# Picking 1024 columns by one-hot products: data as weights against table as weights (last layer of a two-layer Perceiver block on one core)

## The chip, the cores and the metric

The kernel runs on one core of a Trainium2 chip. The metric is the device time of one execution in microseconds (us). Its engines are TensorE (PE in the profile; its weight loads are shown apart as PEld), VectorE (DVE), ScalarE (ACT), GpSimd (POOL) and the DMA queues, which SyncE (SP) mostly issues.

## What is computed

The input `x` is 2 x 64 tokens of 1024 numbers, held as 128 rows. Five sublayers with a residual each go before the one that this document is about: a quantised product with the context, a state-space layer, a linear layer with low-rank experts, a cross attention and a self attention. The sixth and last is this, cut from the reference (`perm` is a random permutation of the 1024 columns, and the input is `_layernorm(x)`):

```python
def _L1_ffn_ref(x, up, down, perm):          # b*l = 128, h = 16 heads, d = 64, m = 256
    unperm = jnp.argsort(perm)
    t = x.reshape(b * l, Dm)
    t = t[:, perm]
    t = t.reshape(b * l, h, d)
    t = jnp.einsum('bhd,hdm->bhm', t, up)
    t = jax.nn.gelu(t, approximate=False)
    t = jnp.einsum('bhm,hmd->bhd', t, down)
    t = t.reshape(b * l, h * d)
    t = t[:, unperm]
    return t
x = x + _L1_ffn_ref(_layernorm(x, axis=-1), L1_ffn_up, L1_ffn_down, L1_ffn_perm)
```

## The kernel before

Each engine has its own program, written out by hand in one order, and the engines meet through semaphores (`wait_ge` waits, `then_inc` signals). TensorE computes `lhsT.T @ rhs`: the second argument of `pe.matmul` is loaded as weights, the third is the moving data, whose columns stream through. PSUM has 8 banks of 512 fp32 columns, written `psum[:, bank, :]`.

The last sublayer begins when `add_to_x` (L1491, DVE) has added the self attention's output to `x`, in two halves of 512 columns. Then, in the order of the work:

- `center` (L1496, DVE) subtracts the mean and writes `h`. PE turns `h` in 8 transposes of 128 x 128 (`transpose_h(5)`, a helper whose instructions carry L969) into banks 6 and 7, so that a bank holds column tiles of `h` on partitions and the 128 tokens along the columns.
- Since a product in fp32r keeps fewer bits than fp32, the turned data is kept as a sum of two fp32r parts, `split[:, 0]` (high, `left_high`, ACT L698) and `split[:, 1]` (low, `left_low`, DVE L1561), each 8 tiles of 128 columns by 128 tokens.
- Meanwhile `variance(5)` (DVE L1475, L1506, L1507) and `rstd_of(5)` (POOL L574) find `rstd`, one number per token. The normalisation is applied after the pick, since a scale per token and a choice of columns can change places.
- **The pick.** `onehot` is a table of 8 tiles, 128 rows (source columns) by 1024 (picked columns), made long before by DVE (L1859). PE forms `psum[token, picked] = sum over tiles of split.T @ onehot` (L1423): for each half `nh` of the picked columns 8 products with the high part and 8 with the low, 128 tokens as weights and 512 table columns moving, into banks 4 and 5. 32 products in all.
- The result stands with tokens on partitions, so it has to be turned again. ACT (L950, half 0) and DVE (L1964, half 1) copy it to `picked`, times `rstd` on the way, which is one number per partition here. PE transposes 4 tiles of each half (L969), and ACT (L952) and DVE (L1966) copy the turned halves to `gT`.
- `up`: 32 positions in `gT` and the weights, two halves of the array each, 64 products of 64 x 128 (L1439) into banks 0 to 7. The first 32 need `g_lo`, the others `g_hi`. Gelu on ACT (L958), then 64 `down` products (L1447) into banks 0 and 1, which are split again in two fp32r parts (ACT L961, DVE L1976, L1974).
- While that runs, DVE writes the second table over the first (L1969, 8 instructions; it must wait for the pick to be done), and 32 placing products (L1458), of the pick's shape, put the columns back. DVE adds them to `x` (L1985) and two DMAs write the output.

`idle_products` (L975) are products of the identity with itself whose results nobody reads. They stand where PE would otherwise wait.

Of the kernel before, what the change touches and what calls it, by code (L numbers as in the profile page):

```python
# [12 lines left out]
ALU = mybir.AluOpType  # L13
ACT = mybir.ActivationFunctionType
# [7 lines left out]
P = 128  # L22
B, L = 2, 64
D = 1024
KT = D // P
UK = 4
UN = 512
# [62 lines left out]
def perceiver(nc, dram, out):  # L90
# [7 lines left out]
    with ExitStack() as stack:  # L98
        def sb(name, shape, dtype=F32):
            return stack.enter_context(nc.sbuf_tensor(name, shape, dtype))  # L100

        def sem(name):
            return stack.enter_context(nc.semaphore(name))
# [5 lines left out]
        ident = sb("ident", [P, P])  # L109
# [4 lines left out]
        arena = sb("arena", [P, 24576])  # L114
# [4 lines left out]
        split = sb("split", [P, 2, KT, P], F32R)  # L119
        psum = stack.enter_context(nc.psum_tensor("psum", [P, 8, 512], F32))  # L120

        def carve(tile, start, *dims):
            size = 1
            for d in dims:
                size *= d
            ap = tile[:, start:start + size]
            if len(dims) == 2:
                ap = ap.rearrange("p (a b) -> p a b", a=dims[0])
            if len(dims) == 3:
                ap = ap.rearrange("p (a b c) -> p a b c", a=dims[0], b=dims[1])  # L130
            return ap
# [13 lines left out]
        rstd = carve(small, 89, 6)  # L145
# [109 lines left out]
        onehot = carve(arena_r, 15488, KT, D)  # L255
        gT = carve(arena, 0, KT, P)
        hidden = carve(arena, 1024, MH, 2, P)
        picked = carve(arena, 5120, D)
        y_out = carve(arena, 6144, D)


# [23 lines left out]
        rstd_ready = sem("rstd_ready")  # L285
# [119 lines left out]
        pick_ready = sem("pick_ready")  # L405
        place_ready = sem("place_ready")
        g_psum = sem("g_psum")
        picked_lo = sem("picked_lo")
        picked_hi = sem("picked_hi")
        gT_turned = sem("gT_turned")  # L410
        g_lo = sem("g_lo")
        g_hi = sem("g_hi")
        up_psum = sem("up_psum")
# [59 lines left out]
        def place(n):  # L473
            if slot_of[n] > SLOTS:
                return ring_spare[:, slot_of[n] - SLOTS - 1, :]
            return ring_more if slot_of[n] == SLOTS else ring[:, slot_of[n], :]
# [40 lines left out]
        def wide(ap, count):  # L517

            n = ap.shape[1]
            return ap.rearrange("p (u n) -> p u n", u=1).to_broadcast([P, count, n])  # L520
# [143 lines left out]
        def _(act):  # L664
# [16 lines left out]
            for n in range(8):  # L681
# [7 lines left out]
                for cols in code_parts(n):  # L689
                    act.activation(ctx_code[:, n % 2, cols], ring[:, slot_of[n], cols], ACT.Identity, bias=quant[:, 3:4],  # L690
                                   scale=qrec[:, 1:2]).then_inc(ctx_scaled, 1)
# [225 lines left out]
            for r in range(GQ):  # L917
                last = act.activation(krep[:, :, r, :], krot.rearrange("p (g d) -> p g d", g=HKV), ACT.Copy, scale=rstd[:, 4:5])
# [26 lines left out]

            left_high(hT_psum, 10)
            act.preload_act_table_set("gelu_and_others")
            act.wait_ge(g_psum, 1)
            act.wait_ge(rstd_ready, 6)
            act.activation(picked[:, 0:UN], psum[:, 4, :], ACT.Copy, scale=rstd[:, 5:6]).then_inc(picked_lo, 1)  # L950
            act.wait_ge(gT_turned, 1)
            act.activation(gT[:, 0:4, :], psum[:, 6, :], ACT.Copy).then_inc(g_lo, 1)  # L952
            for q in range(4):
                for r in range(2):

# [8 lines left out]
        def _(pe):  # L964
            def transpose4(bank, tile, first_col, signal):

                for k in range(4):
                    c = first_col + P * k
                    last = pe.transpose(psum[:, bank, P * k:P * k + P], tile[:, c:c + P], ident[:, :])  # L969
                last.then_inc(signal, 1)  # L970
# [11 lines left out]
            for nh in range(2):  # L982
                for kh in range(2):
                    for b in range(B):
# [3 lines left out]
                        for k in range(UK):  # L988
# [7 lines left out]
                            last = pe.matmul(psum[rows, 2 + nh, :], ones64, right, **at)  # L996
                last.then_inc(q_done, 1)
            for k in range(UK // 2, UK):
                last = pe.matmul(psum[L:P, 1, :], q1T[:, UK + k, L:P], q2[:, 7, UN * k:UN * k + UN], start=False,
                                 stop=(k == UK - 1))  # L1000
# [256 lines left out]
            for k in range(KT):  # L1257
                last = pe.matmul(psum[:, 4, 0:NE * RANK + NE], hT[:, k, :], w_ar[:, k, :], start=(k == 0), stop=(k == KT - 1))
# [156 lines left out]
            idle_products(0, 4)  # L1415
            transpose_h(5)
            pe.wait_ge(pick_ready, KT)
            for nh in range(2):
                for part, signal in enumerate((hs_high, hs_low)):
                    for k in range(KT):  # L1420
                        if nh == 0 and k % 4 == 0:
                            pe.wait_ge(signal, 9 + k // 4)
                        last = pe.matmul(psum[:, 4 + nh, :], split[:, part, k, :], onehot[:, k, UN * nh:UN * nh + UN],  # L1423
                                         start=(part == 0 and k == 0), stop=(part == 1 and k == KT - 1))
                last.then_inc(g_psum, 1)
            for half in range(2):
                pe.wait_ge(picked_hi if half else picked_lo, 1)
                transpose4(6 + half, picked, UN * half, gT_turned)
            up = place(first["mlp_up"]).rearrange("p (a m) -> p a m", a=MH // 2)
            down = place(first["mlp_down"]).rearrange("p (m h d) -> p m h d", m=2, h=MH)  # L1430
            arrived(pe, first["mlp_up"])
# [1 line left out]
            for a in range(MH // 2):  # L1433
                pe.wait_ge(g_hi if a >= 4 else g_lo, 1)
                for m in range(2):
                    for r in range(2):
                        rows = slice(MD * r, MD * r + MD)
                        at = 256 * (a % 2) + P * m
                        last = pe.matmul(psum[:, 4 * r + a // 2, at:at + P], up[rows, a, P * m:P * m + P], gT[rows, a, :],  # L1439
                                         start=True, stop=True)  # L1440
                if a % 2:
                    last.then_inc(up_psum, 1)
            for a in range(MH // 2):
                pe.wait_ge(hidden_ready, 2 * (a // 2 + 1))
                for m in range(2):
                    for r in range(2):
                        last = pe.matmul(psum[MD * r:MD * r + MD, a // 4, P * (a % 4):P * (a % 4) + P], down[:, m, 2 * a + r, :],  # L1447
                                         hidden[:, 2 * a + r, m, :], start=(m == 0), stop=(m == 1))
                if a % 4 == 3:
                    last.then_inc(down_psum, 1)  # L1450
            for nh in range(2):
                for part, signal in enumerate((o_high, o_low)):
                    for k in range(KT):
                        if nh == 0 and k % 4 == 0:
                            pe.wait_ge(signal, k // 4 + 1)
                        if nh == 0 and part == 0:
                            pe.wait_ge(place_ready, k + 1)
                        last = pe.matmul(psum[:, 2 + nh, :], split[:, part, k, :], onehot[:, k, UN * nh:UN * nh + UN],  # L1458
                                         start=(part == 0 and k == 0), stop=(part == 1 and k == KT - 1))
# [3 lines left out]
        def _(dve):  # L1463
# [7 lines left out]
            def halves(nh):  # L1471
                return slice(UN * nh, UN * nh + UN)
# [16 lines left out]
            def add_to_x(nh, bank, factor=1.0):  # L1489

                dve.scalar_tensor_tensor(out=x[:, halves(nh)], in0=psum[:, bank, :], scalar=factor, in1=x[:, halves(nh)],  # L1491
                                         op0=ALU.mult, op1=ALU.add, accum_out=x_sum[:, nh:nh + 1]).then_inc(x_ready, 1)
                updates[0] += 1
                dve.wait_ge(x_ready, updates[0])
# [6 lines left out]
            def variance(n):  # L1501

                statistics(0)
                statistics(1)
                dve.wait_ge(stats_ready, 2 * n + 2)
                step(dve.bn_aggr(mv, stats.rearrange("p a b -> p (a b)")))  # L1506
                dve.tensor_scalar(var_eps, mv[:, 1:2], LN_EPS, None, ALU.add).then_inc(var_ready, 1)  # L1507
# [135 lines left out]
            for i, (a, c) in enumerate(parts):  # L1643
                last = dve.tensor_scalar(rms_var[:, i:i + 1], rms_sum[:, i:i + 1], 1.0 / (c - a), RMS_EPS, ALU.mult, ALU.add)
# [308 lines left out]
            low(25)  # L1953
            for nh in range(2):
                dve.wait_ge(ao_psum, nh + 1)
                add_to_x(nh, 4 + nh)


            center()
            left_low(10)  # L1960
            variance(5)
            dve.wait_ge(g_psum, 2)
            dve.wait_ge(rstd_ready, 6)
            dve.tensor_scalar(picked[:, halves(1)], psum[:, 5, :], rstd[:, 5:6], None, ALU.mult).then_inc(picked_hi, 1)  # L1964
            dve.wait_ge(gT_turned, 2)
            dve.tensor_copy(gT[:, 4:8, :], psum[:, 7, :]).then_inc(g_hi, 1)  # L1966

            for k in range(KT):
                dve.tensor_scalar(onehot[:, k, :], iota, perm_col[:, k:k + 1], None, ALU.is_equal).then_inc(place_ready, 1)  # L1969
# [93 lines left out]
```

## Time and profile before

| | us |
|---|---|
| median of 3 runs (359.96 to 360.26) | 360.2 |
| the profiled execution, its own time | 359.97 |
| its span, first to last instruction | 358.1 |
| PE busy in it | 323.7 (90%) |
| DVE busy | 268.1 (75%) |
| ACT busy | 205.4 (57%) |

The profile describes one execution. Its span is 1.9 us shorter than the time of the same execution, which holds what lies around the instructions. A busy time of an engine adds the stretches in which it worked on something; a matmul's recorded length contains the trip of the data through the array, so a row of matmuls overlaps itself and its pace has to be read from start to start. "idle before" is how long an engine sat before the instruction, and "<-" names what ended that.

### The profile page before, as it was taken

The numbers are of one execution on the slowest core, as the hardware profiler recorded it, in microseconds if no ns is written. First come the engines' busy times: TensorE is split into PE (matmuls) and PEld (weight loads), VectorE is DVE, ScalarE is ACT, GpSimd is POOL, SyncE is SP. The second block draws the span as 40 slices with busy tenths as digits, with TensorE's granted clock in tenths as the row PEclk, the third lists the DMA queues.
The fourth block names the chain that finished last, engine by engine and source line by source line (L and its number), as shares of the span: only waits on it lengthen the run. The fifth ranks groups of instructions, "written<-read, shape, count | busy, mean of one in ns | idle before, by whom it ended". The sixth has DMA issues, their size and how long they took to land.

```text
span 358.1 us, 5132 instructions
## 1 busy us (share of the span) xinstructions
PE 323.7 (90%) x1944; PEld 214.5 (60%) x1944; DVE 268.1 (75%) x369; ACT 205.4 (57%) x402; POOL 108.7 (30%) x75
## 2 busy tenths in 40 slices
PE   0697999999789999999899898999999999898996
PEld 0344564654456566667548776785343777777794
DVE  1877787768788999999594998995423898875381
ACT  1984644168999999997425735651024566451250
POOL 2510100042987999999200020202000110400000
PEclk9999999999999999999999999999999999999999
DMA  6999999945003021363579696789999993000001
GB/s 238 424 423 417 422 319 420 385 158 195 12 0 118 2 71 49 118 240 117 165 285 372 254 422 263 282 348 373 417 425 357 428 419 137 4 2 0 0 2 59
DMA packets 12966, 81.85 MB, mean 229 GB/s; under 512 B 2109, under 2 KB 2365, under 8 KB 3661
## 3 DMA queue, kind: packets, MB, share of 16 engines
q1 hardware_dynamic: 11614, 78.23, 55.9%
q10 hardware_dynamic: 1296, 3.22, 2.6%
q8 instruction: 15, 0.25, 0.3%
q14 instruction: 9, 0.07, 0.1%
q0 software_dynamic: 32, 0.07, 0.1%
HBM read 80.86 MB, written 0.52 MB: 227 GB/s over the span
## 4 chain that ended last, share of the span: by engine, by line
PE 44%; DVE 16%; ACT 2%; issue 2%; POOL 1%; DVEq 0%
PE psum L1012 8%; PE psum L1304 8%; PE psum L1019 4%; PE psum L1189 4%; PE psum L1149 4%; DVE rounded L1752 4%; PE psum L1224 3%; PE psum L1073 3%; PE psum L969 2%; PE psum L1423 2%; PE psum L1458 2%; DVE arena L1690 1%; DVE arena_halves L1760 1%; PE psum L1439 1%; PE psum L1447 1%
## 5 line engine op out<-in xcount | busy, mean ns | idle before, releaser
L800 ACT ACTIVATE arena<-arena 128x126 f32<-128x126 f32 x256 | 75.9, 392 | 0.3 <-DVE plain L1690 0.3
L635 POOL TENSOR_TENSOR arena<-arena 128x1024 f32<-128x1024 f32 x21 | 49.7, 2377 | 11.8 <-DVE arena L1690 10.7
L1690 DVE TENSOR_TENSOR_SCAN arena<-arena,psum 128x1024 f32<-128x1024 f32 x22 | 49.7, 2275 | 1.7 <-PE psum L1149 1.3
L1073 PE MATMUL psum<-ring,hT 128*128 128x512 f32 x104 | 50.2, 605 | 0.8 <-ACT hT L701 0.8
L574 POOL TENSOR_TENSOR small<-small 128x1 f32<-128x1 f32 x6 | 9.6, 1607 | 135.0 <-DVE small L1507 129.4
L1752 DVE TENSOR_TENSOR rounded<-ring,rounded 128x2048 fp32r<-128x2048 f32 x16 | 36.5, 2286 | 15.0 <-ACT rounded L827 15.0
L827 ACT ACTIVATE rounded<-ring 128x2048 fp32r<-128x2048 f32 x16 | 30.6, 1913 | 17.5 <-PE psum L1019 9.5
L1189 PEld LDWEIGHTS psum<-ident,arena 128*128 128x128 f32 x256 | 28.9, 141 | 12.5 <-issue 12.1
L1189 PE MATMUL psum<-ident,arena 128*128 128x128 f32 x256 | 33.6, 275 | 0.0
L1149 PE MATMUL psum<-rounded 64*128 64x512 f32 x192 | 30.9, 426 | 1.7 <-DVE arena L1690 1.0
L1073 PEld LDWEIGHTS psum<-ring,hT 128*128 128x128 f32 x104 | 17.8, 190 | 17.6 <-issue 16.4
L1012 PE MATMUL psum<-rounded,split 128*128 128x512 f32 x96 | 24.6, 399 | 2.4 <-DVE rounded L1752 1.8
L1304 PE MATMUL psum<-ring,arena 128*64 128x512 f32 x96 | 24.4, 593 | 0.0
L635 POOL TENSOR_TENSOR arena<-plain,arena 128x1024 f32<-128x1024 f32 x10 | 23.7, 2374 | 0.9 <-DVE plain L1690 0.7
L1690 DVE TENSOR_TENSOR_SCAN plain<-arena,psum 128x1024 f32<-128x1024 f32 x10 | 22.8, 2276 | 0.4 <-ACT arena L800 0.3
L969 PE MATMUL psum<-ident,arena 128*128 128x128 f32 x120 | 18.7, 280 | 4.0 <-DVE arena L1662 1.7
L1149 PEld LDWEIGHTS psum<-rounded 64*128 64x128 f32 x192 | 15.6, 185 | 10.7 <-issue 5.2
L1012 PEld LDWEIGHTS psum<-rounded,split 128*128 128x128 f32 x96 | 17.5, 188 | 7.5 <-DVE rounded L1752 2.9
L690 ACT ACTIVATE arena<-ring,small 128x2048 uint8<-128x2048 f32 (+1 forms) x9 | 16.9, 1900 | 7.9 <-DMA ring<-in_ctx 7.9
L969 PE MATMUL psum<-ident,h 128*128 128x128 f32 x48 | 7.4, 304 | 15.1 <-DVE h L1518 11.7
L969 PEld LDWEIGHTS psum<-ident,arena 128*128 128x128 f32 x120 | 13.4, 140 | 11.7 <-issue 6.0
L827 ACT ACTIVATE arena_halves<-ring 128x2048 fp32r<-128x2048 f32 x8 | 15.3, 1917 | 6.1 <-PE psum L1019 5.6
(238 smaller groups left out, 574.9 us busy)
## 6 DMA issues: line engine op xcount, KB each, us to landing
ring<-in_w_in SPq DMA_DIRECT2D x16, 1024.0 KB, 15.2
ring<-in_ctx SPq DMA_DIRECT2D x13, 1024.0 KB, 10.2
ring<-in_w_out SPq DMA_DIRECT2D x8, 1024.0 KB, 5.1
ring<-in_ctx_t SPq DMA_DIRECT2D x7, 1024.0 KB, 5.6
ring<-in_w_base SPq DMA_DIRECT2D x4, 1024.0 KB, 4.9
ring<-in_x_wk SPq DMA_DIRECT2D x4, 1024.0 KB, 10.2
ring<-in_a_wo SPq DMA_DIRECT2D x4, 1024.0 KB, 11.8
ring<-in_x_wq SPq DMA_DIRECT2D x3, 1024.0 KB, 9.0
```

The lines of the kernel that those rows point to most:

```text
L635: pool.tensor_tensor(product[s % STATES].rearrange("p (n b t) -> p b n t", n=HN, b=B), state[s % STATES].rearrange("p (b n t) -> p b n t", ...
L690: act.activation(ctx_code[:, n % 2, cols], ring[:, slot_of[n], cols], ACT.Identity, bias=quant[:, 3:4], scale=qrec[:, 1:2]).then_inc(ctx_s ...
L800: last = act.activation(to, of, ACT.Exp, scale=a_par[:, k, state_no:state_no + 1])
L827: act.activation(unit_halves[m % 3][:, 0, :, :], slot(split_units[m]), ACT.Copy).then_inc(unit_high, 1)
L969: last = pe.transpose(psum[:, bank, P * k:P * k + P], tile[:, c:c + P], ident[:, :])
L1012: pe.matmul(psum[:, bank, :], left(0, k0 + k), unit[:, w, k, :], start=(start and k == 0 and w == 0), stop=False)
L1073: last = pe.matmul(psum[:, proj_bank(j), :], hT[:, k, :], slot(w_in + u)[:, k % UK, :], **at)
L1149: last = pe.matmul(psum[:, input_bank(s, b), :], du[k // GD][rows_of(b), a, left], bdiag[rows_of(b), w, right, :], start=(n == 0), stop=(n ...
L1189: last = pe.matmul(psum[:, y_bank(q), to:to + P], product[s % STATES][:, P * n:P * n + P], ident[:, :], start=(s % 2 == 0 and n == 0), sto ...
L1304: last = pe.matmul(psum[L * b:L * b + L, bank, :], left[:, UK * kh + k, L * b:L * b + L], slot(u0 + b)[:, k, :], start=(kh == 0 and k == 0 ...
L1690: dve.tensor_tensor_scan(state[s % STATES], dA[:, s % 3, :], psum[:, p:p + 2, :].rearrange("p a b -> p (a b)"), 0.0, ALU.mult, ALU.add).th ...
L1752: dve.tensor_tensor(unit[:, 1, :, :], slot(split_units[m]), unit[:, 0, :, :].bitcast(F32), ALU.subtract).then_inc(unit_low, 1)
```

## The change

The operands of the pick change places. A table tile of 128 x 128 is now the weights, and the turned data (one tile of 128 tokens) moves through it. What comes out stands already turned, with picked columns on partitions and tokens along the columns. So `picked`, its two scaled copies and the 8 transposes go, and for each half, part and tile there are now 4 products of 128 columns in place of 1 of 512: 128 in all, into banks 2 and 3.

The scale `rstd` now belongs to a column, not to a partition. DVE writes a diagonal of it (`rstd_diag`, from the identity), PE multiplies a 128 x 128 matrix of ones with it (one product into bank 7, between the halves of the pick), ACT copies the result to `rstd_wide`, and DVE multiplies each half of the pick by it on the way to `gT`. The ones are written by a memset on DVE before the first `add_to_x`.

```diff
-            for nh in range(2):
+            for half in range(2):
                 for part, signal in enumerate((hs_high, hs_low)):
                     for k in range(KT):
-                        if nh == 0 and k % 4 == 0:
+                        if half == 0 and k % 4 == 0:
                             pe.wait_ge(signal, 9 + k // 4)
-                        last = pe.matmul(psum[:, 4 + nh, :], split[:, part, k, :], onehot[:, k, UN * nh:UN * nh + UN],
-                                         start=(part == 0 and k == 0), stop=(part == 1 and k == KT - 1))
+                        for m in range(4):
+                            of = UN * half + P * m
+                            last = pe.matmul(psum[:, 2 + half, P * m:P * m + P], onehot[:, k, of:of + P], split[:, part, k, :],
+                                             start=(part == 0 and k == 0 and m == 0), stop=(part == 1 and k == KT - 1),
+                                             skip_group_check=True)
                 last.then_inc(g_psum, 1)
-            for half in range(2):
-                pe.wait_ge(picked_hi if half else picked_lo, 1)
-                transpose4(6 + half, picked, UN * half, gT_turned)
+                if half == 0:
+                    pe.wait_ge(diag_ready, 2)
+                    pe.matmul(psum[:, 7, 0:P], all_ones, rstd_diag, start=True, stop=True).then_inc(g_psum, 1)
...
             left_high(hT_psum, 10)
             act.preload_act_table_set("gelu_and_others")
-            act.wait_ge(g_psum, 1)
-            act.wait_ge(rstd_ready, 6)
-            act.activation(picked[:, 0:UN], psum[:, 4, :], ACT.Copy, scale=rstd[:, 5:6]).then_inc(picked_lo, 1)
-            act.wait_ge(gT_turned, 1)
-            act.activation(gT[:, 0:4, :], psum[:, 6, :], ACT.Copy).then_inc(g_lo, 1)
+            act.wait_ge(g_psum, 2)
+            act.activation(rstd_wide, psum[:, 7, 0:P], ACT.Copy).then_inc(wide_ready, 1)
...
                 dve.wait_ge(ao_psum, nh + 1)
+                if nh == 0:
+                    dve.memset(all_ones, 1.0).then_inc(diag_ready, 1)
                 add_to_x(nh, 4 + nh)
...
             variance(5)
-            dve.wait_ge(g_psum, 2)
             dve.wait_ge(rstd_ready, 6)
-            dve.tensor_scalar(picked[:, halves(1)], psum[:, 5, :], rstd[:, 5:6], None, ALU.mult).then_inc(picked_hi, 1)
-            dve.wait_ge(gT_turned, 2)
-            dve.tensor_copy(gT[:, 4:8, :], psum[:, 7, :]).then_inc(g_hi, 1)
+            dve.tensor_scalar(rstd_diag, ident[:, :], rstd[:, 5:6], None, ALU.mult).then_inc(diag_ready, 1)
+            for half in range(2):
+                if half == 0:
+                    dve.wait_ge(wide_ready, 1)
+                else:
+                    dve.wait_ge(g_psum, 3)
+                dve.tensor_tensor(gT[:, 4 * half:4 * half + 4, :], psum[:, 2 + half, :].rearrange("p (m t) -> p m t", m=4),
+                                  wide(rstd_wide, 4), ALU.mult).then_inc(g_hi if half else g_lo, 1)
```

PE's rows before, from the last products of the self attention to the placing products:

```order
L975 MATMUL psum<-ident 128x128 x4
L969 MATMUL psum<-ident,h 128x128 x8
L1423 MATMUL psum<-arena_halves,split 128x512 x32
L969 MATMUL psum<-ident,arena 128x128 x8
L1439 MATMUL psum<-arena,ring 128x128 x32
```

The same place with the change (lines of PE's program stand 2 lower up to the pick, 1 higher behind it):

```order
L973 MATMUL psum<-ident 128x128 x4
L967 MATMUL psum<-ident,h 128x128 x8
L1423 MATMUL psum<-split,arena_halves 128x128 x64
L1429 MATMUL psum<-arena 128x128
L1423 MATMUL psum<-split,arena_halves 128x128 x64
L1440 MATMUL psum<-arena,ring 128x128 x32
```

Forty instructions (32 products, 8 transposes) became 129, all of 128 moving columns, and each has a weight load of 128 columns.

DVE before, from `variance(5)` to the second table, with the semaphores that it waits on:

```order
L1507 TENSOR_SCALAR small<-small 128x1 [waits dve_step]
L1964 TENSOR_SCALAR arena<-psum,small 128x512 [waits rstd_ready,g_psum]
L1966 COPY arena<-psum 128x512 [waits gT_turned]
L1969 TENSOR_SCALAR arena_halves<-arena,small 128x1024 x8
L1976 TENSOR_TENSOR split<-psum,split 128x512 [waits o_high]
```

And with the change:

```order
L1508 TENSOR_SCALAR small<-small 128x1 [waits dve_step]
L1966 TENSOR_SCALAR arena<-ident,small 128x128 [waits rstd_ready]
L1972 TENSOR_TENSOR arena<-psum,arena 128x512 [waits wide_ready]
L1972 TENSOR_TENSOR arena<-psum,arena 128x512 [waits g_psum]
L1976 TENSOR_SCALAR arena_halves<-arena,small 128x1024 x8
L1983 TENSOR_TENSOR split<-psum,split 128x512 [waits o_high]
```

DVE now writes both halves of `gT`, and the second table comes behind one instruction that follows the pick where two did.

## Rows read from the trace of the kernel before

**Rows 1.** The page: busy times, granted clock, chain that ended last

```profile
PE 323.7 (90%) x1944; PEld 214.5 (60%) x1944; DVE 268.1 (75%) x369; ACT 205.4 (57%) x402; POOL 108.7 (30%) x75
...
PEclk9999999999999999999999999999999999999999
```

**Rows 2.** Chain of waits, end of the kernel: start us, us, what

```profile
328.00 0.71 DVE x L1491 x2
...
329.53 0.67 PE psum L969 x4
...
330.22 0.61 ACT split L698
...
330.96 7.55 PE psum L1423 x32
...
338.54 0.76 DVE arena L1964
...
339.35 0.66 PE psum L969 x4
340.00 3.77 PE psum L1439 x64
...
347.42 7.50 PE psum L1458 x32
```

**Rows 3.** Timeline, 318 to 359 us: start us, us, instruction [idle before]

```profile
325.20 0.69 DVE L1491 SCALAR_TENSOR_TENSOR x<-psum,x 128x512 f32<-128x512 f32 x1 [1.15 <-PE psum L1019]
...
328.00 0.69 DVE L1491 SCALAR_TENSOR_TENSOR x<-psum,x 128x512 f32<-128x512 f32 x1 [2.10 <-PE psum L1019]
...
330.96 7.54 PE L1423 MATMUL psum<-arena_halves,split 128*128 128x512 f32 x32 [0.34 <-ACT split L698]
...
333.84 0.55 POOL L574 TENSOR_TENSOR small<-small 128x1 f32<-128x1 f32 x1 [21.66 <-DVE small L1507]
...
339.93 3.84 PE L1439 MATMUL psum<-arena,ring 64*128 64x128 f32 x64
340.04 0.69 DVE L1966 COPY arena<-psum 128x512 f32<-128x512 f32 x1 [0.75 <-PE psum L969]
340.65 5.39 DVE L1969 TENSOR_SCALAR arena_halves<-arena,small 128x1024 fp32r<-128x1024 f32 x8
...
346.42 0.69 DVE L1976 TENSOR_TENSOR split<-psum,split 128x512 fp32r<-128x512 f32 x1 [0.38 <-ACT split L961]
```

**Rows 4.** Timeline of PE, 66 to 72 and 200 to 318 us

```profile
67.21 2.81 PE L1089 MATMUL psum<-arena 128*128 128x96 f32 x24
...
207.42 2.02 PE L1258 MATMUL psum<-arena,hT 128*128 128x136 f32 x16
217.90 1.05 PE L975 MATMUL psum<-ident 128*128 128x128 f32 x8
...
306.04 2.05 PE L975 MATMUL psum<-ident 128*128 128x128 f32 x16
```

**Rows 5.** Groups by line and shape, PEld: busy us, mean ns | idle before

```profile
L1012 PEld LDWEIGHTS psum<-rounded,split 128*128 128x128 f32 x96 | 17.5, 188 | 7.5 <-DVE rounded L1752 2.9 <-ACT split L698 1.2
...
L969 PEld LDWEIGHTS psum<-ident,arena 128*128 128x128 f32 x120 | 13.4, 140 | 11.7 <-issue 6.0 <-ACT arena L937 1.3 <-ACT arena L902 1.0
...
L1089 PEld LDWEIGHTS psum<-arena 128*128 128x128 f32 x32 | 3.9, 192 | 1.0 <-issue 0.6 <-DVE arena L1618 0.3
```

**Rows 6.** One line each: durations ns min/median/max, first and last start us

```profile
L878 ACT ACTIVATE arena<-psum x1: 277/277/277, 214.8 to 214.8; 128x128 f32<-128x128 f32 x1
...
L1713 DVE SCALAR_TENSOR_TENSOR arena<-arena,small,psum x16: 322/340/346, 115.0 to 182.3; 128x128 f32<-128x128 f32 x16
...
L995 PEld LDWEIGHTS psum<-arena x30: 106/110/178, 14.5 to 28.8; 128*64 128x64 bf16 x30
```

**Rows 7.** Stretches: us, busy (x) of PE, PEld, DVE, ACT, POOL, PEclk, DMA, GB/s

```profile
300.00:307.00 7.00, 6.72 (x153) 5.78 (x152) 6.70 (x10) 1.44 (x2) 0.00 (x0) 1.00 0.02 5
...
331.00:338.50 7.50, 7.50 (x34) 6.16 (x35) 2.69 (x6) 2.28 (x3) 0.55 (x1) 1.00 0.00 0
```

More of the change, by code:

```diff
@@ L257, in perceiver @@
         hidden = carve(arena, 1024, MH, 2, P)
-        picked = carve(arena, 5120, D)
+        all_ones = carve(arena, 5120, P)
+        rstd_diag = carve(arena, 5248, P)
+        rstd_wide = carve(arena, 5376, P)
         y_out = carve(arena, 6144, D)
@@ L407, in perceiver @@
         g_psum = sem("g_psum")
-        picked_lo = sem("picked_lo")
-        picked_hi = sem("picked_hi")
-        gT_turned = sem("gT_turned")
+        diag_ready = sem("diag_ready")
+        wide_ready = sem("wide_ready")
         g_lo = sem("g_lo")
```

## The prediction

> **What bounds the kernel now.** I read the page first. PE is busy for 90% of the span and the granted clock is at its full level in every slice, which is the 2.4 GHz one of TensorE's two levels [rows 1]. A busy share does not say which engine ends a stage, so the next view is the chain of waits over the last sublayer [rows 2]. The reader is to see that it is one string without gaps: DVE adds and centres, PE turns `h` (0.67 us), ACT makes the high part (0.61), PE picks (7.55 from 330.96), DVE scales the second half (0.76), PE turns it (0.66), then the `up` products start (340.00) and, behind the `down` products, the placing products (7.50 from 347.42). The timeline has the first `up` product at 339.93 [rows 3]; I count from this time. From the first picking product to the first `up` product it is **339.93 - 330.96 = 8.97 us**, and this is the piece that the change rewrites. No transfer ends a wait in this piece, and nothing before it or behind it in PE's order is edited.
>
> **What the change takes away.** The second scaled copy, the second four transposes and the steps between go from the chain. The pick's last product ends at 338.52 (330.96 + 7.55, rounded), so this is 339.93 - 338.52 = 1.4 us. The first half's copy and transposes were hidden behind PE and DVE already and are worth nothing by themselves. If 128 products took as long as 32 did, the change would win these 1.4 us.
>
> **What a product costs now.** The question is the pace of a 128-column load followed by a product of 128 moving columns in fp32r. No row of before has that pair, so I bound it.
>
> - The old products run at (7.54 - 0.39)/31 = 0.23 us from start to start (0.39 is the recorded length of one) [rows 3]. That is 512 columns of data, and the load was hidden behind them. A quarter of it, 0.057 us, is what 128 columns would take if only the moving data counted: the **lower end**.
> - Products in fp32 with 128-column loads show what the load does. 24 products with 96 moving columns take 2.81 us: (2.81 - 0.275)/23 = 0.110 each. 8 with 128 columns: (1.05 - 0.275)/7 = 0.111. 16 with 136 columns: (2.02 - 0.279)/15 = 0.116 [rows 4]. From 128 to 136 the pace grows with the data. From 96 to 128 it does not: fewer columns bought nothing. Something that does not depend on the moving data takes 0.110 us, and what these three have in common is the load of 128 fp32 columns.
> - Is a load of fp32r as dear as one of fp32? Their records are as long: 188 ns on average for fp32r tables and data, 192 for fp32 [rows 5]. The record follows the work: a bf16 load of 64 columns has a median of 110 ns [rows 6] and the load of a transpose 140 ns [rows 5]. So a shorter load would be seen, and fp32r does not show one. I take **0.110 us** for a pair: the moving part (0.057) hides behind the load, where before the load hid behind the moving part.
> - The upper end. If load and moving part could not overlap, a pair would take 0.110 + 0.057 = 0.167 us. If a short product cost as much as a long one whatever its columns, it would be 0.23.
>
> Nearest among these is the row of 96 columns, a full-width load with less moving work than load work, which is the new pair's situation. A stretch of 16 idle products runs at (2.05 - 0.275)/15 = 0.118 [rows 4], so the pace of long runs is not always the best one; I allow 0.105 to 0.122.
>
> **The sum.** 128 picking products and the product of ones are 129 pairs: 129 x 0.110 = 14.2 us, in place of 8.97. The first `up` product then starts at 345.15 instead of 339.93: **+5.2 us**. Everything else I cost at nothing on this path, for these reasons.
>
> - The memset of `all_ones` is one small DVE instruction ahead of the first addition. The second addition starts at 328.00 after 2.10 us of idle time [rows 3], so DVE has the room. Without that room it would delay `center` by its own length, and with it the pick.
> - The diagonal: POOL's `rstd` is ready at 333.84 + 0.55 = 334.39 [rows 3]. DVE's scaling of the identity has the size of the 128 x 128 operation at 0.34 us [rows 6], so it is ready at about 334.8. PE asks for it after 64 products, at 330.96 + 7.04 = 338.0. There is no wait. At a pace under 0.06 there would be one of some 0.2 us.
> - ACT's copy to `rstd_wide` is like the 128 x 128 copy at 0.28 us [rows 6], and DVE's multiplication of the first half takes about 0.75 us, as its other PSUM operations of this size with an operand do [rows 2]. Both lie under the second half of the pick. The first half of `gT` is ready at about 339.4, well before 345.15.
> - The second half of `gT` is late by design: DVE starts it when the last picking product ends, about 0.16 us after the first `up` product starts, and is done 0.95 us after that start. Only the 33rd `up` product needs it, which comes after half of 3.84 us, 1.9 us. It is hidden.
> - The second table: DVE wrote it from 0.72 us to 6.11 us after the first `up` product [rows 3]. Now it goes from 0.95 to about 6.35. The next DVE step, the subtraction for the low part, came at 346.42, 6.49 us after the first `up` product, because it waited for ACT. The margin is 0.14 us; a worse DVE delay would be paid once, at its own size.
> - ACT's and DVE's other savings (L952, L966's place, L950) free engines that are not what PE waits for.
>
> A rule of the Trainium skill speaks for the change. "TensorE: Matmul & The Clock Gate", section "Weight-path perf modes — Fast Weight Load (FWL) and DoubleRow", says that loads of 128 weights in a type other than fp32 take a fast path, about twice as quick. By it a pair would take about 0.057 us and the sum would be a gain of 1.4 us. The equal records of fp32r and fp32 above are why the forecast does not go by it.
>
> **The numbers.** The sum is made on the profiled execution: 358.1 + 5.2 = 363.3 us of span, 359.97 + 5.2 = 365.2 us of time. That execution is 0.2 us under the median of the runs shown, so the median should come out at 360.2 + 5.2 = **365.4 us**. The allowance of 0.105 to 0.122 gives 13.5 to 15.7 us, or +4.6 to +6.8: 364.8 to 367.0. Differences under 0.2%, 0.7 us, can't be told from no change.
>
> **The rivals.**
>
> - *The load hides too (faster).* The mechanism is a quick load of fp32r tables in front of 128-column products. The `up` products show such a pace, (3.84 - 0.27)/63 = 0.057 us a product with 128-column loads [rows 3], but there two halves of the array take turns, and here each product needs the whole array. The first half would end at 334.6, the product of ones would wait for the diagonal until 334.8, and the second half would end at 334.8 + 65 x 0.057 = 338.5: 1.4 us earlier, **358.8 us**. It decides from a pace of 8.97/129 = 0.070 us downward. For it speaks that 512-column products say nothing on a load's true price, only that it is under 0.23. Against it stand the records of 188 ns. Chance 12%.
> - *Half-way.* The load is partly quicker, with a pace in the middle between 0.057 and 0.110, 0.084 us: 129 x 0.084 = 10.8 us, +1.9, **362.1 us**. Chance 6%. The same page of the Trainium skill, section "Back-to-back issue gap", gives about 81 ns for a load and a product of 128 columns, which would make it 361.7 us.
> - *No overlap.* Every table tile has to be in the whole array before its data moves, and the next load waits until the data is through: 129 x 0.167 = 21.5 us, +12.6, **372.8 us**. Against it: fp32 products of 128 columns have at least as much moving work and run at 0.111, which leaves no room for a sum. Chance 6%. The same page of the Trainium skill, section "The mechanism", says that a load overlaps running products only when its row group differs, which would give this case; the rows just named speak against it.
> - *A short fp32r product is as dear as a long one.* 129 x 0.23 = 29.7 us, +20.7, **380.9 us**. No fp32r product with under 512 moving columns is in the trace, so nothing excludes it, but fp32 ones got cheaper with their columns. Chance 5%.
> - *The clock falls.* PE moves fewer columns per us in the new stretch. In 300 to 307 us, 153 products, most of 64 columns, ran with the full clock granted [rows 7], as the old pick did. At the lower level the tail behind the pick would take up to twice as long. Chance 1%.
>
> **How the numbers follow.** The forecast, a pace set by the load, has 70%. The range reaches from the half-way case with its rounding, 361.3, to the case without overlap, 373.0. It leaves out the faster case (12%) and the two dearest (6%). Faster by over 0.2% is the first rival and a little of the half-way one, 13%; within 0.2% is a pace of 0.064 to 0.075, 2%; slower is the rest, 85%.
>
> **What would show it.** In the profile after: 128 products at the pick's line over about 14.1 us, load records still near 188 ns and nearly back to back, the first `up` product near 345.1, clock 1.00 throughout. The product of ones should show no wait for DVE, ACT's copy of it should lie under the pick, and from the first `up` product to the end everything should look as before, with the same 18.1 us. If the pick's products come at 0.06 us, the step from the load records to the load's price was wrong; if they come well above 0.12, either the overlap or the price of short fp32r products was. If the pace is right and the time is not, the tail behind the first `up` product has grown, and the second table or the second half of `gT` is where to look.

## The result, and the profile after

The median of 4 runs with the change is 366.2 us (366.03 to 366.22), against 360.23 us (359.96 to 360.28) for 4 runs of the kernel before. The ratio is 1.0167, with a 95% interval from 1.0155 to 1.0178: **1.7% slower, 6.0 us**. The prediction said 365.4 us, in a range of 361.3 to 373.0.

The profiled execution of the changed kernel took 366.03 us, with a span of 364.0. Its page, the counterpart of [rows 1]:

```profile
span 364.0 us, 5311 instructions
...
PE 330.9 (91%) x2034; PEld 223.2 (61%) x2034; DVE 268.4 (74%) x371; ACT 204.4 (56%) x401; POOL 108.7 (30%) x75
...
PEclk9999999999989999999999999999999999999999
```

Read alone, these lines hide the change: PE's busy share went from 90% to 91%. The chain of waits from 329 us on (start us, us, what) shows where the time is; it answers [rows 2]:

```profile
329.76 0.67 PE psum L967 x4
...
330.45 0.60 ACT split L699
...
331.20 7.33 PE psum L1423 x64
338.53 0.27 PE psum L1429 x2
338.80 7.10 PE psum L1423 x64
345.90 3.77 PE psum L1440 x64
349.67 3.64 PE psum L1448 x64
353.32 7.48 PE psum L1459 x32
```

Before, the pick was one row of 7.55 us, followed by 0.76 on DVE and 0.66 of transposes. Now the last picking product is followed at once by the `up` products, as the change intends, but the two rows of the pick hold 14.4 us. The timeline of the changed kernel, 323 to 365 us, has the rest (it answers [rows 3]):

```profile
325.50 0.17 DVE L1958 MEMSET arena<- 128x128 f32 x1 [1.22 <-PE psum L1017]
...
328.24 0.69 DVE L1492 SCALAR_TENSOR_TENSOR x<-psum,x 128x512 f32<-128x512 f32 x1 [2.02 <-PE psum L1017]
...
331.17 7.22 PEld L1423 LDWEIGHTS psum<-split,arena_halves 128*128 128x128 f32 x64 [0.55 <-issue]
331.20 7.33 PE L1423 MATMUL psum<-split,arena_halves 128*128 128x128 f32 x64 [0.34 <-ACT split L699]
...
334.66 0.29 DVE L1966 TENSOR_SCALAR arena<-ident,small 128x128 f32<-128x128 f32 x1 [0.66 <-POOL small L575]
338.31 0.30 PEld L1429 LDWEIGHTS psum<-arena 128*128 128x128 f32 x2
338.37 0.44 PE L1429 MATMUL psum<-arena 128*128 128x128 f32 x2
...
338.84 0.28 ACT L950 ACTIVATE arena<-psum 128x128 f32<-128x128 f32 x1 [6.00 <-PE psum L1429]
339.15 0.69 DVE L1972 TENSOR_TENSOR arena<-psum,arena 128x512 f32<-128x512 f32 x1 [4.20 <-ACT arena L950]
345.83 3.65 PEld L1440 LDWEIGHTS psum<-arena,ring 64*128 64x128 f32 x64
345.83 3.84 PE L1440 MATMUL psum<-arena,ring 64*128 64x128 f32 x64
345.94 0.69 DVE L1972 TENSOR_TENSOR arena<-psum,arena 128x512 f32<-128x512 f32 x1 [6.10 <-PE psum L1423]
346.55 5.38 DVE L1976 TENSOR_SCALAR arena_halves<-arena,small 128x1024 fp32r<-128x1024 f32 x8
```

Three readings. The loads (PEld) stand as long as the products, 7.22 beside 7.33 us: the load engine's record has no gap left. The pace is (7.33 - 0.28)/63 = 0.112 us. And from the first picking product to the first `up` product it is 345.83 - 331.20 = **14.63 us, against 8.97 before: 5.66 us** of the 5.9 by which the span grew. Behind that point nothing moved: 364.0 - 345.83 = 18.2 us, as before.

The other 0.24 us lie ahead of the pick. They came up between 102 and 199 us: a row of products of an earlier sublayer starts at 101.86 us here and at 101.89 before, an addition of DVE at 199.17 here and at 198.96 before. The change edits nothing there. The slice with an 8 in the clock's line is a short fall of the granted clock, which one row of the stretches places (us, busy of PE, PEld, DVE, ACT, POOL, PEclk, DMA, GB/s):

```profile
103.00:106.00 3.00, 3.00 (x13) 2.06 (x13) 1.42 (x2) 2.94 (x8) 1.09 (x2) 0.60 0.00 0
```

In this profile the clock was at the lower level for part of that stretch. The profile of before had 1.00 there, although PE had been busy for as long in 100 to 103 us (1.21 us before, 1.20 here). Of 11 runs of the kernel before, made beside a later experiment, 9 had a mean clock of 0.994 to 0.998 where its profile has 1.000, one had 1.000, and one had 0.947 and took 364.31 us. So the kernel before meets this fall too, and once a much longer one (an estimate from the mean: (1 - 0.947)/0.5 x 362.4 = 38 us at the lower level). The fall need not be all of the 0.24 us: a later version that kept a clock of 1.000 began its pick at 331.13 us, and another, which is the kernel before up to the pick, at 331.39.

### The profile page after: what moved, and what is told of

Its sections match the earlier page's. It is cut to its first block, busy times and chain, and to the rows that moved or that the text cites. A ratio compares the mean times of both kernels' runs of the same rounds, so it can differ in the third digit from the quotient of the medians.

```text
span 364.0 us, 5311 instructions
## 1 busy us (share of the span) xinstructions
PE 330.9 (91%) x2034; PEld 223.2 (61%) x2034; DVE 268.4 (74%) x371; ACT 204.4 (56%) x401; POOL 108.7 (30%) x75
## 4 chain that ended last, share of the span: by engine, by line
PE 59%; DVE 17%; issue 8%; ACT 7%; DMA 6%; POOL 2%; SPq 0%; DVEq 0%; ACTq 0%; POOLq 0%
PE psum L1010 8%; PE psum L1302 8%; PE psum L1071 7%; PE psum L1187 6%; DMA ring<-in_ctx 6%; PE psum L1147 6%; PE psum L1017 4%; PE psum L1423 4%; DVE rounded L1753 3%; PE psum L967 3%; PE psum L1222 3%; ACT arena L801 2%; PE psum L1459 2%; DVE arena L1691 2%; DVE arena_halves L1761 1%
```

## A correction to the counting ahead

The text ahead speaks of 64 `up` products and 64 `down` products. The loops make 32 of each, and the trace shows 64 records of each: a product of plain fp32 leaves two matmul records with two loads here. A product of fp32r leaves one record, and so does a transpose (8 for 8). `idle_products(0, 4)` is 8 records in the same way. The paces of [rows 4] are paces of records, each with its load, so the price of a load stands. The product of ones is fp32, though, and it is the row "L1429 ... x2" above. The prediction counted it once.

## The experiments

All seven leave the work ahead of the last sublayer as it is. The question is what the 0.112 us are the price of: the load, the moving columns, or a product as such. The first four were executed once each, beside one execution of the kernel before that took 360.5 us; they are read by their paces, and only roughly by their times.

**Half of the moving columns.**

```diff
-last = pe.matmul(psum[:, 2 + half, P * m:P * m + P], onehot[:, k, of:of + P], split[:, part, k, :],
+last = pe.matmul(psum[:, 2 + half, P * m:P * m + L], onehot[:, k, of:of + P], split[:, part, k, 0:L],
```

> The changed kernel, but each of the 128 picking products moves 64 tokens instead of 128; the weight load keeps its 128 columns. It leaves out the pick for the second batch. Theory (the load of 128 fp32r columns sets the pace): 0.112 us from start to start as in the changed kernel, time 366.2 us. Rival A (short fp32r products pay double per moving column, 128 of them 0.107 us, and the load hides behind): 0.055 us, 128 x 0.055 less, about 359 us. Rival B (a fixed price for every product, whatever its operands): 0.112 us and 366.2 us, as the theory.

Measured: 379.28 us, 13 us more than any theory gave. The stretches of this run (columns as above):

```profile
331.50:333.50 2.00, 2.00 (x19) 2.00 (x19) 2.00 (x4) 1.61 (x2) 0.00 (x0) 1.00 0.00 0
...
333.50:335.00 1.50, 1.50 (x14) 1.50 (x14) 0.77 (x4) 0.00 (x0) 0.55 (x1) 0.86 0.00 0
335.00:338.00 3.00, 3.00 (x16) 3.00 (x16) 0.24 (x1) 0.00 (x0) 0.00 (x0) 0.50 0.00 0
...
347.00:351.00 4.00, 4.00 (x20) 4.00 (x21) 0.00 (x0) 0.00 (x0) 0.00 (x0) 0.50 0.00 0
```

While the clock was at 2.4 GHz there were 19 products in 2.0 us, 0.105 us each (0.10 to 0.11, since whole products are counted): halving the moving columns bought next to nothing, so the moving part does not set the pace (rival A falls). Then, between 333.5 and 335 us, the granted clock went to 0.50, the 1.2 GHz level, and the pace to 4.0/20 = 0.20 us. The total time of this run is that of a lower clock and says nothing on the question; only the first 2 us do.

**Half of the loaded columns.**

```diff
-last = pe.matmul(psum[:, 2 + half, P * m:P * m + P], onehot[:, k, of:of + P], split[:, part, k, :],
+last = pe.matmul(psum[0:L, 2 + half, P * m:P * m + P], onehot[:, k, of:of + L], split[:, part, k, :],
```

> The changed kernel, but each picking product loads 64 table columns instead of 128 and moves 128 tokens. It leaves out half of the picked columns. Theory (the load sets the pace): the load halves, 0.055 to 0.06 us a product, 128 x 0.055 = 7 us less, about 359 us. Rival A (the moving part, double per column): 0.107 to 0.112 us, 366.2 us. Rival B (a fixed price): 0.112 us, 366.2 us.

Measured: 359.69 us, beside 360.5 us for the kernel before on the same chip. The chain of waits and the line's own view (ns min/median/max):

```profile
331.39 4.02 PE psum L1423 x64
335.41 0.28 PE psum L1429 x2
335.69 3.84 PE psum L1423 x64
```

```profile
L1423 PEld LDWEIGHTS psum<-split,arena_halves x128: 133/136/138, 331.4 to 339.2; 128*64 128x64 f32 x128
L1423 PE MATMUL psum<-split,arena_halves x128: 220/223/302, 331.4 to 339.3; 128*64 128x128 f32 x128
```

With the same 128 moving columns and the same number of products, 3.84/64 = 0.060 us each. Half the load, half the price, and nearly as low as the moving columns allow (the 0.057 us of the prediction's lower end). Rival A and rival B, the fixed price, both fall here.

**The same bytes as bf16.**

```diff
-last = pe.matmul(psum[:, 2 + half, P * m:P * m + P], onehot[:, k, of:of + P], split[:, part, k, :],
+last = pe.matmul(psum[:, 2 + half, P * m:P * m + P], onehot[:, k, of:of + L].bitcast(BF16),
+                 split[:, part, k, 0:L].bitcast(BF16),
```

> The changed kernel, but the same bytes are read as bf16: each product loads 128 bf16 columns and moves 128 bf16 columns, half of the bytes. The numbers picked are not the reference's. If the price of the load hangs on the type (a bf16 load of 64 columns was 110 ns long in the trace before where an fp32 one was 137): 0.055 to 0.06 us a product, about 359 us. If any load of 128 columns costs the same: 0.112 us, 366.2 us.

Measured: 359.36 us.

```profile
L1423 PEld LDWEIGHTS psum<-split,arena_halves x128: 95/98/100, 331.3 to 339.0; 128*128 128x128 bf16 x128
```

```profile
335.66 3.57 PE psum L1423 x64
```

128 columns loaded, 128 moved, and 3.57/64 = 0.056 us. So it is not the number of columns alone: the type, or the bytes behind it, halves the pace. Both operands changed here, but the moving one did not set the pace before. And 0.056 us is about the 0.057 that the prediction worked out for 128 moving columns by themselves, so it is the most that the bf16 load can cost; its own price may be lower. The load's record is 98 ns long, where the changed kernel has this:

```profile
L1423 PEld LDWEIGHTS psum<-split,arena_halves x128: 186/192/192, 331.2 to 345.6; 128*128 128x128 f32 x128
```

This is the pace that the prediction's first rival needed. It exists, for bf16. The fast path of the Trainium skill ("TensorE: Matmul & The Clock Gate", section "Weight-path perf modes — Fast Weight Load (FWL) and DoubleRow") is given there to loads of 128 weights in a type other than fp32. These two rows fit it if fp32r is counted as fp32; whether the bf16 loads took that path no row tells.

**The old roles, cut to 128 columns.**

```diff
-                        last = pe.matmul(psum[:, 4 + nh, :], split[:, part, k, :], onehot[:, k, UN * nh:UN * nh + UN],
-                                         start=(part == 0 and k == 0), stop=(part == 1 and k == KT - 1))
+                        for m in range(4):
+                            of = UN * nh + P * m
+                            last = pe.matmul(psum[:, 4 + nh, P * m:P * m + P], split[:, part, k, :], onehot[:, k, of:of + P],
+                                             start=(part == 0 and k == 0 and m == 0), stop=(part == 1 and k == KT - 1),
+                                             skip_group_check=True)
```

> The kernel before with its old roles (turned data as weights, table moving) and its transposes, but the 32 products of 512 table columns are cut into 128 products of 128, each with its own load. Theory (the load sets the pace, whichever operand is loaded): 0.112 us a product, 128 x 0.112 + 0.16 = 14.5 us in place of 7.55, 6.95 us slower than before: 367.2 us. Rival C (the load of the table is what is slow, since its rows are far apart, and a load of the data is quick): 0.057 us a product and 360.2 us.

Measured: 367.37 us, 6.9 us over the 360.5 us of the kernel before beside it, forecast 6.95. In its chain:

```profile
331.39 14.49 PE psum L1425 x128
...
345.91 0.76 DVE arena L1967
...
346.71 0.66 PE psum L969 x4
347.37 3.77 PE psum L1442 x64
```

The timeline shows a load for every product:

```profile
331.36 14.37 PEld L1425 LDWEIGHTS psum<-arena_halves,split 128*128 128x128 f32 x128 [0.55 <-issue]
```

The pace, (14.48 - 0.28)/127 = 0.112 us, is that of the changed kernel although the weights are the data, not the table, and although four products in a row load the same tile. What is loaded does not matter; that a load comes with every 128 moving columns does. This run also splits the change in its two effects: the cut from 32 to 128 products costs 6.9 us, and the new roles give 1.3 of them back (from the pick's start to the `up` products the chain has 15.98 us here and 14.70 in the changed kernel).

**Without the product of ones.** PE's product goes and ACT copies the diagonal itself.

```diff
-                if half == 0:
-                    pe.wait_ge(diag_ready, 2)
-                    pe.matmul(psum[:, 7, 0:P], all_ones, rstd_diag, start=True, stop=True).then_inc(g_psum, 1)
...
-            act.wait_ge(g_psum, 2)
-            act.activation(rstd_wide, psum[:, 7, 0:P], ACT.Copy).then_inc(wide_ready, 1)
+            act.wait_ge(g_psum, 1)
+            act.wait_ge(diag_ready, 2)
+            act.activation(rstd_wide, rstd_diag, ACT.Copy).then_inc(wide_ready, 1)
...
-                    dve.wait_ge(g_psum, 3)
+                    dve.wait_ge(g_psum, 2)
```

> The changed kernel without the product of ones: ACT copies the diagonal itself, so the scale is spread wrongly and the product's place in PE's order is empty. The product shows as two records and 0.27 us in the chain of waits, where the prediction had 0.11. Theory: 0.22 to 0.27 us faster than the changed kernel, 365.9 to 366.0 us. Rival (only one more pair at the load's pace): 0.11 us, 366.1 us.

Measured: 365.88 us (365.78 to 366.09, 6 runs), ratio to the kernel before 1.0147 (1.011 to 1.0183). In its chain the pick is one piece:

```profile
331.13 14.48 PE psum L1424 x128
345.61 3.77 PE psum L1438 x64
```

From the pick's start to the `up` products the chain has 14.48 us, against 345.90 - 331.20 = 14.70 with the product: 0.22 us, twice the prediction's 0.11. Between the medians it is 0.3 us, but the two were not taken beside each other.

**Both parts through one load.** If the load is the price, it should be used for more columns. Here each table tile is loaded once, and high and low part move through it side by side; DVE multiplies and adds the two. (A first version, in which one instruction of DVE was to read both parts from PSUM and add them, gave no time; here each part is multiplied by itself.)

```diff
+            def pick(m, k):
+                bank, at = PICK_AT[m]
+                return pe.matmul(psum[:, bank, at:at + 2 * P], onehot[:, k, P * m:P * m + P], split[:, :, k, :],
+                                 start=(at == 0 and k == 0), stop=(k == KT - 1), skip_group_check=True)
...
```

> The pick keeps the new roles, but each table tile is loaded once and both parts of the data move through it, high and low side by side, 256 columns: 64 products. They go to six banks; for each tile DVE multiplies both parts by the spread deviation and adds them. The second half is picked tile by tile, so that DVE follows. The pick can start only when the first low part is there, 0.7 us later. Theory (the pace is the dearer of a load of 128 fp32r columns, 0.112 us, and the moving part, 256 x 0.226/512 = 0.113 us): 64 x 0.113 = 7.2 us in place of 14.3, less the 0.7: about 6.4 us faster than the changed kernel, 359.8 us, 0.4 us under the kernel before, with 0.3 us of doubt for DVE's longer work at the end. Rival A (short fp32r products pay double per column): 64 x 0.213 = 13.6 us, about 366 us.

Measured: 360.39 us (359.89 to 361.62, 11 runs), ratio to the kernel before 1.0009 (1.0 to 1.0018): level with it, and 5.8 us under the changed kernel.

```profile
331.44 0.70 DVE split L1567
...
332.27 4.07 PE psum L1419 x32
336.35 0.22 PE psum L1430 x2
336.57 3.83 PE psum L1419 x32
340.40 3.87 PE psum L1445 x64
```

The later start is there (DVE's low part is now a step of the chain). The pace came out at 3.83/32 = 0.120 us, not 0.113: with 256 moving columns it is above the price of the load (0.112) and above that of the data (0.113). Why, no run shows. 64 x 0.007 = 0.4 us is the gain that was expected and did not come. Rival A's 366 us is far off.

**Each half in the roles that suit it.** The experiments point to a mixture. Half 0 keeps long products and hides its transposes; half 1, whose transposes nothing hides, takes the new roles with both parts through one load.

```diff
+                    last = pe.matmul(psum[:, 4, :], split[:, part, k, :], onehot[:, k, 0:UN],
+                                     start=(part == 0 and k == 0), stop=(part == 1 and k == KT - 1))
...
+            def pick(m):
+                for k in range(KT):
+                    last = pe.matmul(psum[:, PICK_BANK[m - 4], 0:2 * P], onehot[:, k, P * m:P * m + P], split[:, :, k, :],
+                                     start=(k == 0), stop=(k == KT - 1))
+                last.then_inc(g_psum, 1)
+
+            pick(4)
+            pe.wait_ge(diag_ready, 2)
+            pe.matmul(psum[:, 1, 0:P], all_ones, rstd_diag, start=True, stop=True).then_inc(g_psum, 1)
+            pick(5)
+            pe.wait_ge(picked_lo, 1)
+            transpose4(5, picked, 0, g_psum)
+            pick(6)
+            pick(7)
```

> Each half of the pick in the roles that suit it. Half 0 as in the kernel before (data as weights, 16 products of 512 table columns), so that its copy and its four transposes hide under the rest of the pick. Half 1 in the changed roles, tile by tile, with both parts of the data moving through one load (32 products of 256 columns), so that nothing has to be turned after the last product. The product of ones stands after tile 4, the transposes after tile 5. Theory, from measured paces: 16 x 0.226 + 32 x 0.121 + 0.25 for the product of ones + 4 x 0.11 for the transposes = 8.2 us from the first picking product to the first up product, where the kernel before has 8.97 and the changed kernel 14.63: 0.8 us faster than before, 359.4 us. Rival: the semaphore waits between the pieces, or DVE's three operations per tile and the later second table, eat it up: 360.2 us or more.

Measured: 359.52 us (359.29 to 360.27, 11 runs) against 360.36 us (15 runs) of the kernel before, ratio 0.9981 (0.9972 to 0.9990): 0.8 us faster, as forecast, and of the versions that do the whole work the only one that beats the kernel before. The gain is 0.2%, the size below which the prediction would call nothing a change, but these runs are many, taken beside each other, and the interval leaves out 1.

```profile
331.26 3.89 PE psum L1429 x16
335.15 0.95 PE psum L1435 x8
336.11 0.22 PE psum L1441 x2
336.33 0.95 PE psum L1435 x8
337.29 0.44 PE psum L976 x4
337.72 1.91 PE psum L1435 x16
339.64 3.77 PE psum L1457 x64
```

All of it is PE's own work, one piece behind the other, 8.38 us in this view where [rows 2] has 9.04; no wait for ACT or DVE came in between. So the pick itself gives 0.66 of the 0.84 us between the medians, a little less than the 0.8 forecast; the rest isn't traced.

## Why the prediction was right

- **What a product costs now.** The step that carried the forecast was that the load sets the pace at 0.110 us. It was 0.112, and the four tests of it agree: 0.105 with half of the moving columns, 0.060 with half of the loaded ones, 0.056 in bf16, and 0.112 with the operands in either role.
- **The equal records.** That fp32r loads cost what fp32 loads cost was argued from the length of their records, 188 and 192 ns. The conclusion held, and the two cheap loads have shorter records, 136 and 98 ns. But the length of a record does not give the pace by itself, and the trace of the kernel before could have shown it (the first line's numbers are ns min/median/max):

```profile
L1439 PEld LDWEIGHTS psum<-arena,ring x64: 183/188/189, 339.9 to 343.4; 64*128 64x128 f32 x64
...
338.34 0.60 PE L969 MATMUL psum<-ident,arena 128*128 128x128 f32 x4
```

The `up` loads, in turns into two halves of the array, have records of 188 ns at a pace of 0.057 us; the transposes, whose loads have 140 ns [rows 5], run at (0.60 - 0.273)/3 = 0.109 us, no quicker than products with loads of 192. Taken from the records alone the step would have been luck; the row of 96 moving columns and the experiments are what carry it.

- **The sum.** Forecast +5.2 us, measured 5.66 in the profile's piece. The terms that were mis-sized are two: the pace (128 x 0.002 = 0.26 us) and the product of ones, one pair at 0.110 in the sum and 0.22 to 0.27 in the traces, since it is fp32 and leaves two records. Together they make 0.4 of the missing 0.46 us.
- **The covers.** All held. The second addition still waited 2.02 us behind the memset (0.17 us), PE showed no wait for the diagonal (ready at 334.95, asked for at 338.3), both of DVE's multiplications were hidden, and the tail behind the first `up` product is 18.2 us as it was.
- **The median.** 366.2 against 365.4 us. 0.46 us of the gap are the terms above. The other 0.3 us lie outside the piece and stay open. They are of the size of the clock's fall near 105 us: of 15 later runs of the kernel before, 7 with a clock of 0.999 or 1.000 took 359.96 to 360.14 us and 8 with about 0.994 took 360.26 to 360.49. But the clocks of the four runs behind the 360.23 us are not known, and three of these four, at 360.20 to 360.28, look rather as if they had the fall as well.
- **The rivals.** The quick load did not come for fp32r and did for bf16, and there, as that rival had it, the product of ones had to wait for the diagonal (0.25 us). The half-way case and the 81 ns of the Trainium skill ("TensorE: Matmul & The Clock Gate", section "Back-to-back issue gap") fit neither type here: 112 ns in fp32r, 56 in bf16. No overlap (0.167) and the price of a long product (0.23) are excluded by 0.112. The clock did not fall in the changed kernel's pick. It did in the one run with 64 moving columns; the section on the hardware says how little one run shows of the cause.

## What to carry to other kernels

Count loads as well as products: in fp32r, a product with its own 128-column load took 0.112 us with 128 moving columns, 0.120 with 256 and 0.23 with 512, so the columns beyond the first 128 cost little up to 256. To swap the operands for a result that comes out turned pays only while each load still has enough columns behind it; where it has not, move more data through one load, or swap only the part whose transposes nothing hides. A busy share (90% to 91% here) does not see such a change; the distance between two named instructions does.

## What the runs showed of the hardware that I had not expected

- The granted clock fell while PE's records left no gap. With 128-column loads and 64 moving columns, PE and PEld were busy for all of 331.5 to 335 us, and between 333.5 and 335 the clock went to 0.50. It stayed there through the rest of the pick, which took 25 us in place of 14.6, and through the `up` products (6.32 us in the chain in place of 3.77). The same loads with 128 moving columns kept 1.00. The pace went from 0.105 to 0.20 us, and the run to 379.28 us. That the fewer moving columns brought the clock down is not shown: it is one execution, and the kernel before, with no edit, once lost the clock for long as well (mean 0.947, 364.31 us).
- Four consecutive products with the same weights pay for four loads (128 load records and 0.112 us each in the version with the old roles).
- Elements of half the size brought the pace down as half of the loaded columns did (0.056 and 0.060 us, both close to what the 128 moving columns take). Whether the type or the number of bytes is behind it stays open: no run separated them.
